# Mixture of experts on one core: Gelus kept in PSUM, a list made from fewer sequences, no GpSimd drain, stores between loads

## The chip, the cores and the metric

The kernel runs on one core of a Trainium2 chip. The metric is the device time of one execution in microseconds. All times below are of one core.

## The reference

32 sequences of 128 tokens, each token a row of 128 numbers, pass through two layers, and x is added at the end.

```python
# layer 1, conditioned on the sequence
h = gelu(x @ fc1_w.T + fc1_b)                    # 128 -> 512
shared = h @ fc2_w.T + fc2_b                     # 512 -> 96
expert_x = h @ experts_w[indices].T + experts_b  # 512 -> 32, one of 16 experts per sequence
y = concatenate([shared, expert_x])
# layer 2, conditioned on the token
scores = y @ router_w.T                          # 8 experts
top_v, top_i = top_k(scores, 2); routing_w = softmax(top_v)
for e in range(8):
    w_e = sum(where(top_i == e, routing_w, 0))
    out = out + (gelu(y @ expert_w1[e].T) @ expert_w2[e].T) * w_e
return x + out
```

All is float32; the Gelus are exact ones.

## The kernel before

**Pieces.** Layer 1 and the routing run over 16 pieces of two sequences. Per piece TensorE multiplies up (`up`), ScalarE makes the Gelu, TensorE multiplies down, DVE adds the biases (`y_first`), TensorE turns and scores, DVE finds the two best experts (`choose`, `mark`), and `place_pairs` gives each of the two copies of a row its slot in the DRAM tensor `slots`, where every expert has a room of its own. GpSimd writes the rows to their slots, four indirect transfers (scatters) a piece, 64 in all (L519).

**Tiles.** Layer 2 runs over 23 tiles of rows that all belong to one expert: 16 wide ones of 512 rows and 7 narrow ones of 256, in the order wide 0 to 11, narrow 12 and 13, wide 14 to 17, narrow 18 to 22. Which expert and which slots a tile has is found at run time by DVE, in lists: the first three tiles come from the first list, made when 10 pieces are placed, the next four from the second, made on 14 pieces (28 sequences), the rest from the third, made on all. `LIST_PIECE` and `LIST_WIDE` hold these numbers. `early_counts` and `early_list` make the first two lists, `last_counts`, `last_list`, `narrow_list`, `own_tiles`, `needed_tiles` and `counted_signals` the later ones, as chains of small DVE operations placed between the tiles' work (tiles 2, 3, 4, 5, 6 to 9 and 10).

**SP's queue** fetches: for each tile the rows (`pick`, from `slots`) and the expert's weights (`load_weights`, SBUF to SBUF, four buffers), in order. Before the first pick of a list it waits until the scatters of that list's pieces have landed. It writes the eight fillers (rows behind each expert's last one) in threes behind tiles 4, 5 and 6, and the first pick of the third list waits for all of them.

**One tile.** float32 products are made of three passes of float32r: each operand is split into a high and a low part, on both sides. `turn_in` transposes the picked rows into PSUM; ScalarE casts the high part (`picked_high`), DVE subtracts it for the low one (`picked_low`). `tile_up(t, g)` fills half g of `hp` (PSUM, two halves of 1024 columns), six matmuls of 512 columns. ScalarE makes the Gelu from hp into `hs_raw` in SBUF (`tile_gelu`), casts its high part into `hs` (`tile_high`), DVE subtracts it from hs_raw for the low part (`tile_low`, L854). `tile_down` multiplies down, again in halves. DVE copies the result (`flat`), TensorE turns it (`turn_out`), DVE scales the rows by the routing weight (`rows_of`), and GpSimd scatters them into the DRAM tensor `results` (L527), four scatters for a wide tile and two for a narrow one. The last three tiles take one pass and ScalarE does flat and rows_of.

TensorE's order in tile t: up(t, 0), turn_in(t + 1), down(t - 1, 0), up(t, 1), turn_out(t - 2), down(t - 1, 1). DVE's: flat(t - 2), low(t - 1, 1), picked_low(t + 1), low(t, 0), rows_of(t - 2), then a piece of list work. All engines run in written order.

**The end.** In eight chunks SP loads the two results of each token into z when the scatters that this chunk needs have landed (counted at run time, `load_chunk`), DVE adds both and x, SP stores (`store_chunk`). Seven loads come first, then four stores, the eighth load, and the other stores. Then SP waits for all stores and scatters, and all engines meet at a barrier, ahead of which each one drains.

## Time and profile before

| | us |
|---|---|
| median of 3 runs | 238.14 (237.66 to 239.77) |
| the profiled execution | 237.69, its span 235.7 |
| TensorE busy | 203.8 (86%) |
| weight loads of TensorE | 175.3 (74%) |
| DVE busy | 166.6 (71%) |
| ScalarE busy | 143.4 (61%) |
| GpSimd busy | 166.9 (71%) |
| chain that ended last | GpSimd 35%, DVE 20%, issue 19%, TensorE 15%, DMA 6% |

The span is what the profiler sees from the first to the last instruction; the time of the execution is 2.0 us longer. Busy shares leave out the issue of DMAs, and GpSimd's work here is mostly the issue of scatters: between two of them stand some 0.3 us in which the profile names nothing ("issue"). A line of the timeline gives start and length, the engine, the line of the kernel, what is written and read, and in brackets how long the engine stood idle before it and what ended that. PE is TensorE, ACT is ScalarE, POOL is GpSimd, SPq is SP's queue. Matmuls overlap: the start of the next one tells more than a length.

### The profile page before, as it was taken

To read this page: it belongs to the slowest core of one execution; us is meant where nothing else is said; L and a number is where in the kernel's file an instruction comes from. 1 tells how busy PE (TensorE), PEld (TensorE's weight loads), DVE (VectorE), ACT (ScalarE), POOL (GpSimd) and SP (SyncE) were. 2 spreads that over 40 slices of the span, in tenths; PEclk is the share of its full clock that TensorE was granted. 3 is DMA by queue.
4 is the path that set the end of the run, shared out by engine and by line. 5 is a ranking of instruction groups with operands and counts; after the bars stand their busy time and mean duration, and the time that the engine had idled before them with its cause. 6 is when DMAs were issued, how large, how long until landed. Compare 5 with 4: busy or idle time off the path is not lost.

```text
span 235.7 us, 4056 instructions
## 1 busy us (share of the span) xinstructions
PE 203.8 (86%) x1259; PEld 175.3 (74%) x1259; DVE 166.6 (71%) x558; ACT 143.4 (61%) x259; POOL 166.9 (71%) x180
## 2 busy tenths in 40 slices
PE   7999999998898684699999999999999999798200
PEld 3899999997797463588878888888978889686100
DVE  1269999998766883359999999997587666455520
ACT  3768978875556745246776666776569764554200
POOL 5437777877777777745766877787777778777730
PEclk9999999999999999599999999999999999999955
DMA  5899793532278811997849777657897589978970
GB/s 172 248 319 285 233 286 95 136 118 85 87 272 278 318 60 34 332 343 271 330 161 356 268 271 254 255 185 250 298 375 266 217 279 332 394 236 253 313 255 0
DMA packets 25799, 56.11 MB, mean 238 GB/s; under 512 B 4872, under 2 KB 11280, under 8 KB 23218
## 3 DMA queue, kind: packets, MB, share of 16 engines
q1 hardware_dynamic: 20800, 47.27, 58.6%
q0 software_dynamic: 4544, 8.54, 10.4%
q8 instruction: 10, 0.16, 0.3%
q10 hardware_dynamic: 434, 0.06, 0.2%
q14 instruction: 11, 0.09, 0.1%
HBM read 22.76 MB, written 13.02 MB: 152 GB/s over the span
## 4 chain that ended last, share of the span: by engine, by line
POOL 35%; DVE 20%; issue 19%; PE 15%; DMA 6%; SPq 1%; POOLq 0%; DVEq 0%
POOL results L527 25%; POOL slots L519 10%; PE dd L983 5%; PE hp L966 3%; DVE hs L854 2%; DVE ffn L841 2%; DMA results<-rows,back_row 2%; DMA z<-results 2%; PE hp L969 2%; PE hp L1010 1%; DVE top_exp L692 1%; DMA picked<-slots 1%; PE misc L1043 1%; DVE rows L867 1%; DMA slots<-y_rows,slot 1%
## 5 line engine op out<-in xcount | busy, mean ns | idle before, releaser
L527 POOL DMA_INDIRECT results<-rows,back_row x78 | 94.1, 1206 | 31.1 <-issue 23.7
L519 POOL DMA_INDIRECT slots<-y_rows,slot x64 | 66.9, 1045 | 25.7 <-issue 18.9
L1033 PE MATMUL hp<-xs,w 128*128 128x512 f32 x192 | 50.5, 398 | 1.6 <-DVE xs L848 1.6
L854 DVE TENSOR_TENSOR hs<-hs_raw,hs 128x1024 fp32r<-128x1024 f32 x36 | 43.9, 1221 | 10.0 <-ACT hs L596 9.8
L588 ACT ACTIVATE hs_raw<-hp 128x1024 f32<-128x1024 f32 x32 | 32.8, 1025 | 29.3 <-PE hp L1033 29.3
L1033 PEld LDWEIGHTS hp<-xs,w 128*128 128x128 f32 x192 | 36.2, 191 | 9.9 <-issue 2.0
L596 ACT ACTIVATE hs<-hs_raw 128x1024 fp32r<-128x1024 f32 x36 | 38.2, 1061 | 0.6
L983 PE MATMUL dd<-cond,hs_raw 128*128 128x128 f32 x256 | 35.5, 282 | 0.0
L983 PEld LDWEIGHTS dd<-cond,hs_raw 128*128 128x128 f32 x256 | 31.6, 192 | 0.3 <-issue 0.2
L545 ACT ACTIVATE hs_raw<-hp,fc_bias 128x256 f32<-128x256 f32 x64 | 26.0, 468 | 4.1 <-PE hp L969 2.2
L1043 PE MATMUL misc<-hs,w 128*128 128x512 f32 x96 | 27.4, 423 | 0.0
L1043 PE MATMUL dd<-hs,w 128*128 128x512 f32 x96 | 26.1, 407 | 1.0 <-DVE hs L854 1.0
L966 PE MATMUL hp<-xs,w 128*128 128x256 f32 x168 | 25.8, 295 | 0.0
L966 PEld LDWEIGHTS hp<-xs,w 128*128 128x128 f32 x168 | 21.7, 189 | 0.0
L1043 PEld LDWEIGHTS dd<-hs,w 128*128 128x128 f32 x96 | 16.9, 189 | 4.4 <-DVE hs L854 1.4
L1043 PEld LDWEIGHTS misc<-hs,w 128*128 128x128 f32 x96 | 17.7, 198 | 3.1
L584 ACT ACTIVATE xs<-dd 128x512 fp32r<-128x512 f32 (+1 forms) x20 | 11.0, 551 | 11.6 <-PE dd L1018 11.5
L1018 PE MATMUL dd<-ident,picked 128*128 128x128 f32 x64 | 10.2, 284 | 5.5 <-DMA picked<-slots 5.4
L1089 PE MATMUL tr<-ident,yT 128*128 128x128 f32 x78 | 12.4, 274 | 2.3 <-ACT yT L603 2.3
L572 ACT ACTIVATE y_rows<-gap 128x2 f32<-128x2 f32 x32 | 4.8, 197 | 15.3 <-DVE gap L697 15.3
L1089 PEld LDWEIGHTS tr<-ident,yT 128*128 128x128 f32 x78 | 9.6, 140 | 5.9 <-ACT yT L603 3.5
L1018 PEld LDWEIGHTS dd<-ident,picked 128*128 128x128 f32 x64 | 8.0, 145 | 7.7 <-DMA picked<-slots 6.1
(154 smaller groups left out, 294.2 us busy)
## 6 DMA issues: line engine op xcount, KB each, us to landing
w<-ffn SPq DMA_DIRECT2D x20, 1024.0 KB, 5.3
picked<-slots SPq DMA_DIRECT2D x16, 264.0 KB, 3.2
ffn_raw<-in_wT SPq DMA_DIRECT2D x8, 512.0 KB, 5.8
z<-results SPq DMA_DIRECT2D x8, 512.0 KB, 4.9
cond<-in_cexpT SPq DMA_DIRECT2D x32, 80.0 KB, 2.4
x_rows<-in_x SPq DMA_DIRECT2D x1, 2048.0 KB, 11.7
out<-z SPq DMA_DIRECT2D x8, 256.0 KB, 4.6
xs_raw<-in_xT SPq DMA_DIRECT2D x7, 256.0 KB, 5.1
```

The source lines that it names most:

```text
L519: pool.indirect_dma_start(out=slots, out_offset=bass.IndirectOffsetOnAxis(ap=slot[:, p, n:n + 1], axis=0), in_=y_rows[:, p % YB, k, r, :], ...
L527: pool.indirect_dma_start(out=results, out_offset=bass.IndirectOffsetOnAxis(ap=back_row[:, t, r:r + 1], axis=0), in_=rows[:, t % RB, r, :] ...
L545: act.activation(hs_raw[:, p % 2, 1, g, cols], hp[:, g, cols], ACT.Gelu, bias=fc1_bias[:, f:f + 1]).then_inc(a_gelu, 1)
L588: act.activation(hs_raw[:, (NP + t) % 2, 1, g, :], hp[:, g, :], ACT.Gelu).then_inc(c_gelu, 1)
L596: act.activation(hs[:, (NP + t) % 2, 0, g, :], hs_raw[:, (NP + t) % 2, 1, g, :], ACT.Copy)\
L854: dve.tensor_tensor(hs[:, u, 1, g, :], hs_raw[:, u, 1, g, :], hs[:, u, 0, g, :].bitcast(F32), ALU.subtract).then_inc(c_lo, 1)
L966: mm = pe.matmul(to, fc1_parts[:, part, f * P:(f + 1) * P], xs[:, c % XB, v, at:at + PER * P], start=m == 0, stop=m == 2)
L983: mm = pe.matmul(dd[:, p % 2, r, :], hs_raw[:, p % 2, 1, g, n * TILE + r * P:n * TILE + (r + 1) * P], weights_at(p, r)[:, :, f, :], start= ...
L1018: mm = pe.transpose(dx[:, r * P:(r + 1) * P], rows_in(t)[:, r, 0:P], ident[:, :])
L1033: mm = pe.matmul(hp[:, g, n * TILE:(n + 1) * TILE], w[:, t % WB, 0, part, f * P:(f + 1) * P], xs[:, (NP + t) % XB, v, :], start=m == 0, st ...
L1043: mm = pe.matmul(results_of[t % 2], w[:, t % WB, 1, part, f * P:(f + 1) * P], hs[:, (NP + t) % 2, v, g, n * TILE:(n + 1) * TILE], start=f ...
L1089: mm = pe.transpose(tr[:, r, :], yT[:, r * P:(r + 1) * P], ident[:, :])
```

## The change

1. The Gelus of tiles 1 to 19 are written back into `hp` instead of into `hs_raw`; `tile_high` and `tile_low` read them there. Tile 0 and the last three still go to SBUF. TensorE may overwrite a half of hp when the low part of the tile before is made (`c_lo`), not when its Gelu is (`c_gelu`).
2. The three passes of a product are taken with the high parts of both sides first; a group starts on the high part of its input and waits for the low part ahead of its third matmul.
3. The block is left without a drain of GpSimd.
4. The second list is made from 13 pieces (26 sequences) in place of 14, and has 3 tiles in place of 4; the third has one more. The first two lists are made ahead of `choose` within a piece, the second one in pieces 14 and 15 in place of after the last. The fillers move one tile earlier.
5. Stores 0 to 3 are issued each after loads 4 to 7.
6. Smaller moves: DVE makes low(t, 0) of a wide tile ahead of picked_low, and of a narrow tile behind rows_of; ScalarE makes high(t, 0) ahead of picked_high.

```diff
-LIST_PIECE = (LAST - 6, LAST - 2, LAST)
-LIST_WIDE = (3, 4, 9)
+LIST_PIECE = (LAST - 6, LAST - 3, LAST)
+LIST_WIDE = (3, 3, 10)
...
+        def up_of(t, g):
+
+            return hp[:, g if wide(t) else t % 2, :]
+
+
+        def gelu_of(t, g):
+            return hs_raw[:, (NP + t) % 2, 1, g, :] if t == 0 or t >= BY_ACT else up_of(t, g)
...
-        block_ctx = ctx.enter_context(nc.Block())
+        block_ctx = ctx.enter_context(nc.Block(no_gpsimd_drain=True))
...
-                    if t == 4:
+                    if t == LIST_START[1]:
                         sp.wait_ge(s_end, 1)
                         sp.sem_inc(s_go, 1)
                         ends_at = registers(end_i[0:1, :], 0, (EXP - 1) * ROOM * UNIT + TOKENS)
-                    if 4 <= t <= 6:
-                        for e in range((t - 4) * 3, min((t - 3) * 3, EXP)):
+                    if n == 1:
+                        for e in range((t - LIST_START[1]) * 3, min((t - LIST_START[1] + 1) * 3, EXP)):
                             write_filler(ends_at[e], e)
...
-            for c in range(CHUNKS - 1):
+
+            for c in range(CHUNKS):
                 load_chunk(c)
-            for c in range(CHUNKS // 2):
-                store_chunk(c)
-            load_chunk(CHUNKS - 1)
+                if c >= CHUNKS // 2:
+                    store_chunk(c - CHUNKS // 2)
             for c in range(CHUNKS // 2, CHUNKS):
                 store_chunk(c)
...
             def tile_gelu(t, g):
                 act.wait_ge(c_up, gelus(t, g))
-                act.activation(hs_raw[:, (NP + t) % 2, 1, g, :], hp[:, g, :], ACT.Gelu).then_inc(c_gelu, 1)
...
+                act.activation(gelu_of(t, g), up_of(t, g), ACT.Gelu).then_inc(c_gelu, 1)
 
             def tile_high(t, g):
                 act.wait_ge(c_gelu, gelus(t, g))
-                act.activation(hs[:, (NP + t) % 2, 0, g, :], hs_raw[:, (NP + t) % 2, 1, g, :], ACT.Copy)\
-                   .then_inc(c_hi, 1)
+                act.activation(hs[:, (NP + t) % 2, 0, g, :], gelu_of(t, g), ACT.Copy).then_inc(c_hi, 1)
...
                 if wide(t):
                     tile_gelu(t, 0)
+                    tile_high(t, 0)
                     picked_high(t + 1)
-                    tile_high(t, 0)
                     tile_gelu(t, 1)
                     tile_high(t, 1)
...
-                dve.tensor_tensor(hs[:, u, 1, g, :], hs_raw[:, u, 1, g, :], hs[:, u, 0, g, :].bitcast(F32),
+                dve.tensor_tensor(hs[:, u, 1, g, :], gelu_of(t, g), hs[:, u, 0, g, :].bitcast(F32),
                                   ALU.subtract).then_inc(c_lo, 1)
...
+                for i in (0, 1):
+                    if p == LIST_PIECE[i] + 2:
+                        early_counts(i)
+                    if p == LIST_PIECE[i] + 3:
+                        early_list(i)
                 if p:
                     choose(p - 1)
                     mark(p - 1)
-                if p == LIST_PIECE[0] + 2:
-                    early_counts(0)
-                if p == LIST_PIECE[0] + 3:
-                    early_list(0)
 
             y_first(LAST)
             picked_low(0)
             place_pairs(LAST - 1)
             choose(LAST)
             mark(LAST)
-            early_counts(1)
+            picked_low(1)
+            tile_low(0, 0)
             place_pairs(LAST)
             dve.tensor_copy(end_i[:, :], run[:, NP, :]).then_inc(s_end, 1)
-            picked_low(1)
-            early_list(1)
-            tile_low(0, 0)
             tile_low(0, 1)
...
                 if wide(t - 1):
                     tile_low(t - 1, 1)
+                if wide(t):
+                    tile_low(t, 0)
                 if t + 1 < BY_ACT:
                     picked_low(t + 1)
-                tile_low(t, 0)
                 if t - 2 < FREE:
                     rows_of(t - 2)
+                if not wide(t):
+                    tile_low(t, 0)
...
-            PASSES = ((0, 1), (1, 0), (0, 0))
+
+            PASSES = ((0, 0), (1, 0), (0, 1))
...
             def tile_up(t, g):
                 if g == 0:
-                    pe.wait_ge(c_xlo, t + 1)
-                    if t - 1 == LATE_WIDE:
-                        pe.wait_ge(c_gelu, gelus(t - 1, 0))
-                elif t:
-                    pe.wait_ge(c_gelu, last_gelu(t - 1))
+                    pe.wait_ge(c_xhi, t + 1)
+                if t == 1:
+                    pe.wait_ge(c_gelu, gelus(0, g))
+                elif t and wide(t - 1):
+                    pe.wait_ge(c_lo, gelus(t - 1, g))
...
                     for m, (part, v) in enumerate(PASSES):
+                        if f == 0 and m == 2:
+                            pe.wait_ge(c_xlo, t + 1)
...
             def tile_down(t, g):
-                pe.wait_ge(c_lo, gelus(t, g))
+                pe.wait_ge(c_hi, gelus(t, g))
                 for n in range(GB):
                     f = g * GB + n
                     for m, (part, v) in enumerate(PASSES):
+                        if n == 0 and m == 2:
+                            pe.wait_ge(c_lo, gelus(t, g))
...
                             weights_of(t + 2)
-                        if g == 1 and n == 0 and m == 1:
-                            pe.wait_ge(c_gelu, gelus(t + 1, 0))
...
             def narrow_up(t):
-                pe.wait_ge(c_xlo if t < BY_ACT else c_xhi, t + 1)
+                pe.wait_ge(c_xhi, t + 1)
+                if wide(t - 1):
+                    pe.wait_ge(c_lo, gelus(t - 1, 0))
...
             tile_up(0, 0)
-            rank(LAST)
             turn_in(1)
             tile_up(0, 1)
+            rank(LAST)
             weights_of(1)
-            pe.wait_ge(c_gelu, 1)
             tile_up(1, 0)
```

SP's queue at the second list, from its wait for the scatters (s_spread) on. Before:

```order
L301 TENSOR_LOAD list_i [waits s_spread12,s_spread13,s_spread11,s_list,s_spread10]
L339 ISA
L339 DMA picked<-slots 128x528
L352 ISA [waits a_up]
L352 DMA w<-ffn 128x2048
L339 ISA
L339 DMA picked<-slots 128x528
L352 ISA [waits c_down]
L352 DMA w<-ffn 128x2048
L301 TENSOR_LOAD end_i [waits s_end]
```

And now:

```order
L305 TENSOR_LOAD list_i [waits s_spread12,s_spread11,s_list,s_spread10]
L343 ISA
L343 DMA picked<-slots 128x528
L356 ISA [waits a_up]
L356 DMA w<-ffn 128x2048
L305 TENSOR_LOAD end_i [waits s_end]
L325 ISA
L325 DMA slots<-filler 128x264
L325 ISA
L325 DMA slots<-filler 128x264
L325 ISA
L325 DMA slots<-filler 128x264
```

The wait for piece 13 is gone from the second list, and the first three fillers stand between the fetches of tile 3 and those of tile 4.

DVE in wide tile 2, up to its scaling of tile 0's rows. Before:

```order
L860 COPY yT<-dd 128x512 [waits c_down]
L854 TENSOR_TENSOR hs<-hs_raw,hs 128x1024 [waits c_hi]
L846 COPY back_row<-picked 128x4 [waits c_xhi]
L848 TENSOR_TENSOR xs<-dd,xs 128x512
L854 TENSOR_TENSOR hs<-hs_raw,hs 128x1024 [waits c_hi]
L867 TENSOR_TENSOR rows<-tr,picked 128x512 [waits c_turn]
```

And now:

```order
L859 COPY yT<-dd 128x512 [waits c_down]
L853 TENSOR_TENSOR hs<-hp,hs 128x1024 [waits c_hi] x2
L845 COPY back_row<-picked 128x4 [waits c_xhi]
L847 TENSOR_TENSOR xs<-dd,xs 128x512
L866 TENSOR_TENSOR rows<-tr,picked 128x512 [waits c_turn]
```

The two low parts (hs) now follow each other, read hp in PSUM and no longer hs_raw in SBUF, and the next tile's rows (xs) come behind them.

TensorE in a wide tile: the second half-up, the turn-out and the second half-down. Before:

```order
L1033 MATMUL hp<-xs,w 128x512 [waits c_gelu]
L1033 MATMUL hp<-xs,w 128x512 x5
L1089 MATMUL tr<-ident,yT 128x128 [waits c_flat]
L1089 MATMUL tr<-ident,yT 128x128 x3
L1043 MATMUL misc<-hs,w 128x512 [waits c_lo]
L1043 MATMUL misc<-hs,w 128x512 [waits s_w3]
L1043 MATMUL misc<-hs,w 128x512 [waits c_gelu]
L1043 MATMUL misc<-hs,w 128x512 x3
```

And now:

```order
L1037 MATMUL hp<-xs,w 128x512 [waits c_lo]
L1037 MATMUL hp<-xs,w 128x512 x5
L1099 MATMUL tr<-ident,yT 128x128 [waits c_flat]
L1099 MATMUL tr<-ident,yT 128x128 x3
L1049 MATMUL misc<-hs,w 128x512 [waits c_hi]
L1049 MATMUL misc<-hs,w 128x512 [waits s_w3]
L1049 MATMUL misc<-hs,w 128x512 [waits c_lo]
L1049 MATMUL misc<-hs,w 128x512 x3
```

The half-up waits for the low part of the tile before instead of its Gelu; the half-down starts on the high part.

## Rows read from the trace of the kernel before

**Rows 1.** The chain of waits from 83 to 96.5: start, length (us), what held it.

```profile
83.70 0.96 POOL slots L519
...
89.25 2.28 DMA slots<-y_rows,slot
...
93.70 2.66 DMA picked<-slots
```

**Rows 2.** The timeline, TensorE: start, length, engine, line, operation, count, idle before.

```profile
89.45 1.52 PE L1033 MATMUL hp<-xs,w 128*128 128x512 f32 x6
...
96.41 1.11 PE L1018 MATMUL dd<-ident,picked 128*128 128x128 f32 x4 [5.44 <-DMA picked<-slots]
...
103.72 0.62 PE L1033 MATMUL hp<-xs,w 128*128 128x512 f32 x2
```

**Rows 3.** Stretches: length, busy time of each engine, TensorE's granted clock, DMA share, GB/s.

```profile
90.00:100.00 10.00, 4.56 (x16) 3.48 (x15) 3.19 (x5) 2.98 (x4) 7.87 (x8) 0.72 0.59 203
```

**Rows 4.** The timeline in a steady tile: DVE, ScalarE and TensorE.

```profile
129.71 1.55 PE L1033 MATMUL hp<-xs,w 128*128 128x512 f32 x6
...
131.47 1.22 DVE L854 TENSOR_TENSOR hs<-hs_raw,hs 128x1024 fp32r<-128x1024 f32 x1
...
132.70 1.06 ACT L596 ACTIVATE hs<-hs_raw 128x1024 fp32r<-128x1024 f32 x1
...
132.93 1.55 PE L1033 MATMUL hp<-xs,w 128*128 128x512 f32 x6
...
134.32 0.60 PE L1089 MATMUL tr<-ident,yT 128*128 128x128 f32 x4
...
136.14 0.62 PE L1033 MATMUL hp<-xs,w 128*128 128x512 f32 x2
```

**Rows 5.** The timeline: subtractions on DVE, and scatters of GpSimd that start inside them.

```profile
86.31 0.68 DVE L848 TENSOR_TENSOR xs<-dd,xs 128x512 fp32r<-128x512 f32 x1
86.32 0.96 POOL L519 DMA_INDIRECT slots<-y_rows,slot  x1 [0.31 <-issue]
...
133.79 1.23 DVE L854 TENSOR_TENSOR hs<-hs_raw,hs 128x1024 fp32r<-128x1024 f32 x1 [0.18 <-ACT hs L596]
133.99 1.89 POOL L527 DMA_INDIRECT results<-rows,back_row  x1 [0.30 <-issue]
```

**Rows 6.** The timeline and then the chain of waits, near the end.

```profile
198.74 1.22 DVE L854 TENSOR_TENSOR hs<-hs_raw,hs 128x1024 fp32r<-128x1024 f32 x1 [1.51 <-ACT hs L596]
...
201.34 0.98 POOL L527 DMA_INDIRECT results<-rows,back_row  x1 [0.52 <-issue]
...
217.12 5.32 DMA results<-rows,back_row
```

**Rows 7.** The last barrier's line: durations in ns, then the start in us.

```profile
L112 POOLq DRAIN  x1: 11092/11092/11092, 224.4 to 224.4; - x1
...
L112 SPq DRAIN  x1: 7/7/7, 230.4 to 230.4; - x1
```

**Rows 8.** The timeline of SP's queue around the fillers.

```profile
95.46 0.81 SPq L352 DMA_DIRECT2D w<-ffn  x1
98.86 3.06 SPq L321 DMA_DIRECT2D slots<-filler  x3
...
111.76 1.39 SPq L321 DMA_DIRECT2D slots<-filler  x2
120.34 0.35 SPq L339 DMA_DIRECT2D picked<-slots  x1
```

**Rows 9.** The timeline: low parts on DVE beside second halves on TensorE.

```profile
106.76 1.22 DVE L854 TENSOR_TENSOR hs<-hs_raw,hs 128x1024 fp32r<-128x1024 f32 x1
106.93 1.55 PE L1033 MATMUL hp<-xs,w 128*128 128x512 f32 x6
...
119.81 1.55 PE L1033 MATMUL hp<-xs,w 128*128 128x512 f32 x6
...
120.49 1.22 DVE L854 TENSOR_TENSOR hs<-hs_raw,hs 128x1024 fp32r<-128x1024 f32 x1
```

More of the change, by code:

```diff
@@ L96, in gelus @@
     return sum(2 if wide(i) else 1 for i in range(t)) + g + 1
-def last_gelu(t):
-    return gelus(t, 1 if wide(t) else 0)
 def wait(eng, sem, value):
@@ L587, in tile_gelu @@
                 act.wait_ge(c_up, gelus(t, g))
-                act.activation(hs_raw[:, (NP + t) % 2, 1, g, :], hp[:, g, :], ACT.Gelu).then_inc(c_gelu, 1)
-            def narrow_gelu(t):
-                act.wait_ge(c_up, gelus(t, 0))
-                act.activation(hs_raw[:, (NP + t) % 2, 1, 0, :], hp[:, t % 2, :], ACT.Gelu).then_inc(c_gelu, 1)
+                act.activation(gelu_of(t, g), up_of(t, g), ACT.Gelu).then_inc(c_gelu, 1)
             def tile_high(t, g):
                 act.wait_ge(c_gelu, gelus(t, g))
-                act.activation(hs[:, (NP + t) % 2, 0, g, :], hs_raw[:, (NP + t) % 2, 1, g, :], ACT.Copy)\
-                   .then_inc(c_hi, 1)
+                act.activation(hs[:, (NP + t) % 2, 0, g, :], gelu_of(t, g), ACT.Copy).then_inc(c_hi, 1)
             def flat(t):
@@ L645, in _ @@
                     picked_high(t + 1)
-                    narrow_gelu(t)
+                    tile_gelu(t, 0)
                     tile_high(t, 0)
@@ L649, in _ @@
                     flat(t - 2)
-                    narrow_gelu(t)
+                    tile_gelu(t, 0)
                     rows_of(t - 2)
@@ L1063, in narrow_up @@
                         for m, (part, v) in enumerate(PASSES):
+                            if f == 0 and m == 2:
+                                pe.wait_ge(c_xlo, t + 1)
                             mm = pe.matmul(narrow_block(hp[:, t % 2, :], f), w[:, t % WB, 0, part, f * P:(f + 1) * P],
@@ L1071, in narrow_down @@
             def narrow_down(t):
-                pe.wait_ge(c_lo if t < BY_ACT else c_gelu, gelus(t, 0))
+                pe.wait_ge(c_hi if t < BY_ACT else c_gelu, gelus(t, 0))
                 for f in range(FB):
@@ L1075, in narrow_down @@
                         for m, (part, v) in enumerate(PASSES):
+                            if f == 0 and m == 2:
+                                pe.wait_ge(c_lo, gelus(t, 0))
                             mm = pe.matmul(results_of[t % 2][:, 0:UNIT], w[:, t % WB, 1, part, f * P:(f + 1) * P],
```

## The prediction, made before the changed kernel was run

> **What bounds the kernel now.** I read the chain of waits first. It is mostly GpSimd: back to back scatters of pieces, then a hop over SP and a pick, then tiles, then back to back scatters of results. Three places decide, and I opened the timeline at each.
>
> First, the middle. The 56th of the 64 slot scatters begins at 89.25, lands 2.28 us later, and SP issues the pick of tile 3 at 93.70, 4.45 us after that scatter began [rows 1]. TensorE has finished the first half of tile 2 at 91.0 and sits idle until 96.41, when tile 3 is there [rows 2]. In the stretch from 90 to 100 its granted clock averages 0.72 [rows 3]; so in part of it the clock stood at the lower of its two levels (1.2 of 2.4 GHz), after a pause of 5.4 us.
>
> Second, the steady tiles. TensorE starts one tile at 129.71, its second half at 132.93 and the next tile at 136.14: 3.22 and 3.21 us, 6.43 a tile, with no pause named between [rows 4]. That is TensorE's own work, so DVE and ScalarE are free there until they are late. GpSimd also takes 6.4 a tile, but not by its own work: a scatter costs 0.98 plus 0.30 of issue [rows 5, 6], and 4 x 1.28 = 5.1. The scatter that starts at 133.99, inside the DVE subtraction of 133.79 to 135.02, takes 1.89 [rows 5]: it ends 0.86 after the subtraction does. The scatter at 86.32 starts inside a subtraction too, but one that reads PSUM (xs from dd), and takes 0.96 [rows 5]. So a DVE operation whose two inputs lie in SBUF holds a scatter up, one with an input in PSUM does not. The Trainium skill (SBUF — State Buffer, SBUF: two separate sides) says the same: VectorE with two SBUF inputs and GpSimd exclude each other on a shared port pair. By that rule, the trace agrees.
>
> Third, the end. The last scatter that a load of z waits for starts at 217.12 and needs 5.32 us to land while stores run; then come a load of z, two additions and one store [rows 6]. SP is through with everything at 230.4, but the span ends at 235.7: GpSimd's DRAIN, 11.09 us long, began at 224.4 and holds the last barrier until 235.5 [rows 7].
>
> **The change, part by part.** The sum is made against the profiled execution, 237.69 us (span 235.7 and 2.0 around it); the median of the runs is 0.45 higher.
>
> *No drain of GpSimd.* SP's own end becomes the end: 235.7 to about 230.5, so 5.2 us. All results have landed by then, since SP waits for them. Bounds: 0, if whatever GpSimd does in those 11 us is waited for elsewhere, and 5.2.
>
> *Second list on 26 sequences.* SP waits for the 52nd scatter in place of the 56th: 83.70 against 89.25 [rows 1], 5.55 us. That scatter is not earlier through anything else, as GpSimd runs back to back before it. It may be later: tile 0 keeps its Gelu in SBUF, and its two all-SBUF subtractions now lie before the 52nd scatter. A start that falls into one waits for up to 1.0, on average half. I take 0.95 for both together (0 to 1.9). Tile 3 then arrives 4.6 us earlier, at 91.8. Will TensorE be there? It is at 91.0 now [rows 2], which is already soon enough. It should be there 1 to 2 us sooner (an estimate), since DVE no longer makes the 19 list operations between the pieces and tile 0's low parts; they go into the last two pieces, partly into waits that DVE has there. So it waits 1 to 3 us instead of 5.4.
>
> *The clock.* From 96.41 to 103.72 stand 7.31 us [rows 2] for a tile less its first half-up; at the full clock that work takes 6.43 - (134.32 - 132.93) = 5.04 [rows 4]. If the shorter pause leaves the clock up, 2.3 us are gained. I take the whole, as 1 to 3 us of idling are much less than the 5.4 before which it fell; the bound is 0.
>
> *The fillers one tile earlier.* They now sit between the pick of tile 3 and that of tile 4 in SP's queue. Three take 3.06 us [rows 8], with the register loads ahead of them 2.6. Pick 4 falls to 6.8 us behind pick 3, and lands about 0.4 after TensorE wants it. The first pick of the third list before came 8.6 us after the last fillers began (111.76 to 120.34) [rows 8]; by the same step it is now some 0.4 late as well. Both lie in front of a larger stall of the same tile (next part), so 0, with up to 1 on the path if transfers are slow.
>
> *Gelus stay in PSUM.* The half of hp is free only when its low part is done: gelu, high, low instead of gelu alone. For g = 0: high runs from 132.70 to 133.76 and low takes 1.22, so the half would be free at 135.0 and is wanted at 136.14 [rows 4]; high also moves ahead of the cast of the next tile's rows. Slack 1.2 or more. For g = 1 DVE's place in line decides. In a steady tile its low ended at 131.47 + 1.22 = 132.69, and the half is wanted at 132.93 [rows 4]: slack 0.24, so about 0.1 in each of four such tiles. Where DVE makes lists in between there is none. Counting for the last list pushed the low of tile 2 to 107.98, and tile 3's second half started at 106.93: 1.05 us of stall now [rows 9]. The narrow list pushed it to 121.71 against 119.81: 1.9 [rows 9], of which some 0.25 were paid before, when the half-down behind it waited for the same low part, so 1.65. The signal counts of tile 10 are like a shorter list, 0.5; the first late wide tile has the same race, 0.2. Sum of losses 3.8, bounds 2 and 6. How long gelu and high take on PSUM is in no row of these; the nearest is high from SBUF to SBUF, 1.06 [rows 4], and I keep that. The 512 wide subtraction from PSUM takes 0.68 [rows 5]; twice that, 1.36, counts its fixed part twice and is the upper bound for the low part, the present 1.22 is the lower, and I take 1.22. The Trainium skill (VectorE: DVE Perf Modes, the TRN2 errata) puts a PSUM source 62 cycles above an SBUF source, 0.065 us; by it the three list tiles would lose some 0.3 us more.
>
> *High parts first* lets a group start two matmuls before the low part is there. A busy TensorE gains nothing from it. The added waits in mid-group cost nothing when they are met: the half whose down has three waits takes 3.21, the half whose down has one 3.22 [rows 4].
>
> *GpSimd set free.* Until tile 15 its scatters only keep pace with TensorE. At the end they decide. Eleven steps lie between the scatters at 201.34 and 217.12 [rows 6]; at 1.28 each they are 14.1, not 15.8. The first starts about 1.5 earlier, since in narrow tiles rows_of now stands ahead of the low part (198.74, 1.22 long, with DVE idle for 1.51 ahead of it) [rows 6]. Less 0.6 for the z additions, which are still all in SBUF: 2.6 us, bounds 1 and 3.5.
>
> *Stores between loads.* Four stores stand in SP's queue between the seventh load and the eighth, beside the scatter whose landing takes 5.32 where one of a slot took 2.28 [rows 1, 6]. Three of them now go earlier, between loads. I take 0.8 (0 to 2.5). Each store waits for an addition three loads back, which was done before; nothing is held.
>
> Sum: 5.2 + 4.6 + 2.3 - 3.8 + 2.6 + 0.8 = 11.7; 237.69 - 11.7 = 226.0, and 226.4 on the scale of the median.
>
> **Rivals.**
> (a) *The clock falls again* in the remaining pause, or scatters collide with tile 0's subtractions in full: 2.3 or a little more is missing, 228.7. For it speaks that a pause of 1 to 3 us is left, with shorter ones just ahead of it; against it, that this is little more than half of the 5.4 at most.
> (b) *The drain is only moved.* GpSimd has work for 9 us after its last scatter, and the program's end may wait for that outside the span: 5.2 missing, 231.6. Nothing in the trace tells.
> (c) *The loop over PSUM becomes the bound*, and the kernel ends slower. For g = 0 the slack is 1.2. To eat the 11.7 over 14 wide tiles, each must lose 0.85, so gelu, high and low together must be 2.05 us longer, 0.7 each on 1.0 to 1.2. The row of a PSUM read (0.68 for 512) speaks against it. At 0.5 each it is 0.3 a tile, 230.5; at 0.8 each it is 1.2 a tile, 243 and slower than before.
> (d) *TensorE gains more than I give*: no list stalls as DVE's idle moments absorb them, and stores help fully: 222.5.
>
> **How the numbers follow.** Forecast 0.55, (a) 0.18, (b) 0.12, (c) 0.06, of which half above 237, (d) 0.09. Its own bounds make the forecast 223.5 to 229. The range takes in (a), (b) and the edge of (d): 222.5 to 231.5. A measurement of this kernel can tell about 1% from no change. Within 1% needs (b) with most of (c): 0.03. Slower 0.03. Faster 0.94.
>
> **What would show each step.** Page: no DRAIN row on GpSimd at the end, and SP's end at the span's end. Timeline: pick of tile 3 near 89, TensorE's transposes of it near 91.8, and a granted clock near 1.00 from 90 to 100. Low parts read hp; scatters from tile 1 on take 0.98 except beside all-SBUF operations, and GpSimd shows idle time waiting for rows. TensorE's waits name DVE's low part before an up: twice over 1 us, at tiles 3 and 5. I am wrong if TensorE's tile takes clearly more than 6.43, if the time around the span grows past 2.0, or if the pause before tile 3 is over 4 us.

## The result and the profile after

The changed kernel takes 228.09 us, the median of four executions (226.1 to 228.23); the kernel before, run beside it, 238.83. The ratio is 0.953, 95% interval 0.947 to 0.958. The profiled execution took 226.10 us against 237.69 before, its span 224.2 against 235.7. The forecast was 226.4, with a range of 222.5 to 231.5 and 0.94 for faster; made against the profiled execution it was 226.0, and that execution took 226.1. Executions of a kernel fall into a fast and a slow state: the ratios, and the medians of the experiments below, are of fast ones, and a ratio is not the plain quotient of two medians.

The head of the page and its chain, of the kernel after:

```profile
span 224.2 us, 4074 instructions
PE 204.3 (91%) x1259; PEld 174.4 (78%) x1259; DVE 166.0 (74%) x558; ACT 143.1 (64%) x259; POOL 150.0 (67%) x180
...
PE 43%; POOL 26%; issue 10%; DVE 10%; DMA 7%; ACT 2%; SPq 1%; POOLq 0%; DVEq 0%
```

TensorE has as much work as before (204.3 us) in a shorter span. GpSimd lost 17 us of busy time (150.0 from 166.9), and TensorE now leads the chain with 43% where it had 15%.

The chain of waits of the kernel after, from the 52nd scatter to tile 3; it answers to [rows 1]:

```profile
83.68 2.27 DMA slots<-y_rows,slot
...
86.11 1.36 SPq L305
...
87.65 2.82 DMA picked<-slots
```

The scatter that SP waits for starts at 83.68, where that scatter already was in the kernel before (83.70), and tile 3 is on TensorE at 90.51 where it was at 96.41. TensorE's timeline there, for [rows 2]:

```profile
88.52 1.62 PE L1037 MATMUL hp<-xs,w 128*128 128x512 f32 x6 [0.60 <-DVE hs L853]
90.51 0.66 PE L1020 MATMUL dd<-ident,picked 128*128 128x128 f32 x4 [0.37 <-DMA picked<-slots]
...
95.57 1.54 PE L1037 MATMUL hp<-xs,w 128*128 128x512 f32 x6
...
99.89 1.65 PE L1037 MATMUL hp<-xs,w 128*128 128x512 f32 x6 [0.94 <-DVE hs L853]
...
114.40 1.66 PE L1037 MATMUL hp<-xs,w 128*128 128x512 f32 x6 [1.06 <-DVE hs L853]
...
153.91 1.65 PE L1037 MATMUL hp<-xs,w 128*128 128x512 f32 x6 [0.56 <-DVE hs L853]
```

The pause is 0.37 us long in place of 5.44, and from 90.51 to 95.57 stand 5.06 us in place of 7.31. The stretch that answers to [rows 3] has the whole clock:

```profile
90.00:100.00 10.00, 8.69 (x44) 6.83 (x44) 7.17 (x23) 7.08 (x8) 7.68 (x8) 1.00 1.02 367
```

The row at 99.89 is the other side. What held it shows on DVE, in the timeline:

```profile
94.99 0.16 DVE L766 TENSOR_TENSOR count<-run,room 128x8 f32<-128x8 f32 x1
...
98.02 0.69 DVE L859 COPY yT<-misc 128x512 f32<-128x512 f32 x1
98.62 2.35 DVE L853 TENSOR_TENSOR hs<-hp,hs 128x1024 fp32r<-128x1024 f32 x2
```

From 94.99 to 98.0 DVE counts for the last list, then comes a copy, and only then the low part that frees half of hp. It ends at about 99.8 and TensorE goes on at 99.89. Over the whole kernel the waits of TensorE read:

```profile
PE hp L1037 <- DVE hs L853: 3.2, 4, 1.1
```

These are the four rows above. The first, 0.60 in tile 2, costs nothing, since TensorE then waits for tile 3's rows anyway. The other three, in tiles 3, 5 and 11, make 2.6 us. The weight loads ahead of them wait too, so the tiles lose more: tile 3 takes 1.2 us more than in the kernel before, tile 4 0.3, tile 5 1.1, tiles 6 to 10 together 0.3 and tile 11 0.8. The steps of tiles 6 to 10 are 6.43 to 6.58 us.

The end, in the chain of waits and in SP's timeline, for [rows 6]:

```profile
210.43 5.73 DMA results<-rows,back_row
...
216.21 4.05 DMA z<-results
```

```profile
209.80 0.36 SPq L448 DMA_DIRECT2D z<-results  x1
210.21 0.46 SPq L452 DMA_DIRECT2D out<-z  x1
210.77 0.37 SPq L448 DMA_DIRECT2D z<-results  x1
211.20 0.54 SPq L452 DMA_DIRECT2D out<-z  x1
216.21 0.36 SPq L448 DMA_DIRECT2D z<-results  x1
```

The last barrier, for [rows 7]; there is no row of GpSimd any more, and SP's stands at the end of the span:

```profile
L108 SPq DRAIN  x1: 7/7/7, 223.9 to 223.9; - x1
```

From the two profiles the 11.5 us of span divide like this:

| place | rows of before, after | gain, us | forecast |
|---|---|---|---|
| tile 3 is turned in | 96.41, 90.51 | 5.9 | 4.6 |
| tile 3 to the next tile's start (clock) | 7.31, 5.06 | 2.25 | 2.3 |
| that start to the first narrow tile | 57.89, 61.65 | -3.8 | -3.8 |
| from there to the last scatter that a load waits for | 55.51, 53.21 | 2.3 | 2.6 |
| its landing | 5.32, 5.73 | -0.4 | +0.8 |
| load, additions, last store | 7.96, 7.74 | 0.2 | 0 |
| SP's end to the end of the span | 5.3, 0.3 | 5.0 | 5.2 |

The third line runs from 103.72 to 161.61 before and from 95.57 to 157.22 after. Each line is a difference of two starts in two executions; another execution of the same kernel moves a line by some tenths, the landing by more.

### The profile page after: what moved, and what is told of

It reads as the page before. It is cut to its first block, busy times and chain, and to the rows that moved or that the text cites. A ratio compares the mean times of both kernels' runs of the same rounds, so it can differ in the third digit from the quotient of the medians.

```text
span 224.2 us, 4074 instructions
## 1 busy us (share of the span) xinstructions
PE 204.3 (91%) x1259; PEld 174.4 (78%) x1259; DVE 166.0 (74%) x558; ACT 143.1 (64%) x259; POOL 150.0 (67%) x180
## 4 chain that ended last, share of the span: by engine, by line
PE 43%; POOL 26%; issue 10%; DVE 10%; DMA 7%; ACT 2%; SPq 1%; POOLq 0%; DVEq 0%
POOL slots L523 24%; PE hp L1037 14%; PE dd L1049 7%; PE misc L1049 7%; PE tr L1099 3%; PE hp L1072 3%; DMA results<-rows,back_row 3%; DVE hs L853 2%; PE dd L1020 2%; POOL results L531 2%; PE hp L971 2%; DMA z<-results 2%; PE hp L1012 1%; PE dd L1086 1%; PE dd L985 1%
## 5 line engine op out<-in xcount | busy, mean ns | idle before, releaser
L531 POOL DMA_INDIRECT results<-rows,back_row x78 | 78.5, 1007 | 41.4 <-DVE rows L866 20.8
L523 POOL DMA_INDIRECT slots<-y_rows,slot x64 | 65.5, 1023 | 25.8 <-issue 18.9
L1037 PE MATMUL hp<-xs,w 128*128 128x512 f32 x192 | 52.0, 407 | 3.2 <-DVE hs L853 3.2
L592 ACT ACTIVATE hp<-hp 128x1024 f32<-128x1024 f32 x34 | 34.3, 1010 | 28.7 <-PE hp L1037 28.7
L853 DVE TENSOR_TENSOR hs<-hp,hs 128x1024 fp32r<-128x1024 f32 x34 | 41.3, 1219 | 12.5 <-ACT hs L596 12.4
L596 ACT ACTIVATE hs<-hp 128x1024 fp32r<-128x1024 f32 x34 | 34.9, 1027 | 1.1
L1049 PE MATMUL misc<-hs,w 128*128 128x512 f32 x96 | 26.2, 408 | 0.0
L1049 PEld LDWEIGHTS misc<-hs,w 128*128 128x128 f32 x96 | 16.8, 189 | 2.9
L866 DVE TENSOR_TENSOR rows<-tr,picked 128x512 f32<-128x512 f32 x16 | 11.0, 686 | 6.3 <-PE tr L1099 6.3
L943 DVE TENSOR_TENSOR z<-z 128x512 f32<-128x512 f32 x8 | 5.5, 692 | 9.7 <-DMA z<-results 9.7
```

The costliest lines, as they stand in the source:

```text
L523: pool.indirect_dma_start(out=slots, out_offset=bass.IndirectOffsetOnAxis(ap=slot[:, p, n:n + 1], axis=0), in_=y_rows[:, p % YB, k, r, :], ...
L531: pool.indirect_dma_start(out=results, out_offset=bass.IndirectOffsetOnAxis(ap=back_row[:, t, r:r + 1], axis=0), in_=rows[:, t % RB, r, :] ...
L592: act.activation(gelu_of(t, g), up_of(t, g), ACT.Gelu).then_inc(c_gelu, 1)
L596: act.activation(hs[:, (NP + t) % 2, 0, g, :], gelu_of(t, g), ACT.Copy).then_inc(c_hi, 1)
L853: dve.tensor_tensor(hs[:, u, 1, g, :], gelu_of(t, g), hs[:, u, 0, g, :].bitcast(F32), ALU.subtract).then_inc(c_lo, 1)
L1037: mm = pe.matmul(hp[:, g, n * TILE:(n + 1) * TILE], w[:, t % WB, 0, part, f * P:(f + 1) * P], xs[:, (NP + t) % XB, v, :], start=m == 0, st ...
```

## The experiments

again, drain, sbuf_late and sbuf_early ran on one chip, where the kernel before took 238.61. The others ran in three groups on three other chips, where it took 261.8, 268.5 and 265.9. What was different there is told with nodrain. The changed kernel itself was run only where the kernel before takes 238 us.

**again: the changed kernel once more.**

> The changed kernel once more, beside which the others of this group are read. All theories: 226 to 228 us, 0.953 of the kernel before. If the 2 us between its fast and its slow executions have a place in the trace, a second profile may show it: the start of tile 3 (90.51 us in the first profile), or the landing of the last scatter (5.73 us).

227.55 us, ratio 0.952 (0.947 to 0.958): the same. It executed in 225.4 to 228.4, so a single execution says no more than some 1.5 us to either side. Its profiled execution (227.63) shows a wait that the first one had almost without:

```profile
PE dd L1020 <- DMA picked<-slots: 2.2, 2, 2.0
```

TensorE was ready for tile 3 2.0 us early and stood still for that long, yet tile 3 came at 90.67, and the granted clock from 90 to 100 was 1.00 again. In sbuf_early below the pause was 2.96 us, with the same 1.00. In the kernel before the clock fell inside the pause of 5.44 and was 0.50 from 95 to 101.

Why the pause was 0.37 in one profile and 2.03 in the other shows earlier, where TensorE makes the halves of tile 0. The stretch from 78 to 81, the first profile and then again:

```profile
78.00:81.00 3.00, 3.00 (x10) 2.42 (x10) 0.97 (x4) 2.33 (x5) 2.09 (x3) 0.50 1.01 416
```

```profile
78.00:81.00 3.00, 3.00 (x17) 2.08 (x16) 1.25 (x3) 2.98 (x4) 2.39 (x3) 1.00 0.89 361
```

In the first profile the clock fell here, though from 66 on TensorE had stood still for no more than 0.58 us at a time. Tile 2 was turned in 1.8 us later than in again (83.21, 81.42), of which 0.4 were there before the fall. The pause ahead of tile 3 took that up, so tile 3 came no later for it. sbuf_late has the same fall, from about 77 to 80; drain and sbuf_early have not. So a short pause ahead of tile 3 doesn't by itself promise the whole clock: what made it fall at 78 stays open.

**drain: the changed kernel with GpSimd's drain.**

```diff
-        block_ctx = ctx.enter_context(nc.Block(no_gpsimd_drain=True))
+        block_ctx = ctx.enter_context(nc.Block())
```

> The changed kernel with the drain of GpSimd put back. Theory (the drain only held the last barrier): the span is 5.0 us longer than that of the changed kernel, since SP was done at 230.4 of 235.7 before and is done at 223.9 of 224.2 now. Rival (GpSimd's work after its last scatter is waited for anyway, outside the span): the time is the same and only the part outside the span, 1.9 us, shrinks.

232.86 us, ratio 0.976 (0.971 to 0.981), 5.3 above again. Its last barrier:

```profile
L108 POOLq DRAIN  x1: 10837/10837/10837, 218.9 to 218.9; - x1
...
L108 SPq DRAIN  x1: 7/7/7, 224.6 to 224.6; - x1
```

SP is through at 224.6 and GpSimd's row lasts until 229.7, with the span's end at 230.0. The drain is wholly at the end and does nothing that anyone waits for: shown.

**sbuf_late: Gelus in SBUF, TensorE's waits as in the changed kernel.** It undoes the place alone.

```diff
-            return hs_raw[:, (NP + t) % 2, 1, g, :] if t == 0 or t >= BY_ACT else up_of(t, g)
+            return hs_raw[:, (NP + t) % 2, 1, g, :]
```

> The changed kernel with all Gelus in SBUF again, and every wait as in the changed kernel (TensorE still waits for the low part). So only the place of the Gelu differs. Theory (two SBUF inputs on DVE hold a scatter up): the 78 scatters of results take 94 us in sum, not 78.5, GpSimd no longer waits for rows (20.8 us now), and the end is 1 to 2 us later, as the lag of GpSimd counts only at the end. Rival 1 (scatters are slowed by the transfers they compete with, not by DVE): 78 to 80 us in sum as now. Rival 2 (GpSimd's pace bounds the whole stretch): 6 us or more later.

228.25 us, ratio 0.956 (0.951 to 0.961): 0.7 above again, with intervals that overlap. The scatters of results, on the page of sbuf_late and then of the changed kernel:

```profile
L531 POOL DMA_INDIRECT results<-rows,back_row x78 | 91.3, 1171 | 28.0 <-issue 21.3
```

```profile
L531 POOL DMA_INDIRECT results<-rows,back_row x78 | 78.5, 1007 | 41.4 <-DVE rows L866 20.8
```

A scatter is issued in 1.17 us on average instead of 1.01, 13 us in all. The timelines show it one by one, sbuf_late first:

```profile
132.54 1.22 DVE L853 TENSOR_TENSOR hs<-hs_raw,hs 128x1024 fp32r<-128x1024 f32 x1
132.75 1.86 POOL L531 DMA_INDIRECT results<-rows,back_row  x1 [0.30 <-issue]
```

```profile
127.83 1.22 DVE L853 TENSOR_TENSOR hs<-hp,hs 128x1024 fp32r<-128x1024 f32 x1 [0.47 <-ACT hs L596]
128.67 0.98 POOL L531 DMA_INDIRECT results<-rows,back_row  x1 [0.30 <-issue]
```

Inside a subtraction of two SBUF inputs the scatter lasts until 134.61, 0.85 after the subtraction; inside one that reads hp it takes its 0.98. The one edit between the two kernels is where the Gelu lies, so the stretching is shown to come from it. In time the two kernels differ by less than their executions spread: the intervals leave room for some 2 us, and exclude the 6 of the second rival. Most of the 13 us turns into idle time: GpSimd waits 20.8 us for DVE's rows in the changed kernel and 4.9 in sbuf_late.

**sbuf_early: Gelus in SBUF, and TensorE waits for the Gelu only.** The edit of sbuf_late, and with it

```diff
-                if t == 1:
-                    pe.wait_ge(c_gelu, gelus(0, g))
-                elif t and wide(t - 1):
-                    pe.wait_ge(c_lo, gelus(t - 1, g))
+                if t:
+                    pe.wait_ge(c_gelu, gelus(t - 1, g if wide(t - 1) else 0))
...
                 if wide(t - 1):
-                    pe.wait_ge(c_lo, gelus(t - 1, 0))
+                    pe.wait_ge(c_gelu, gelus(t - 1, 0))
```

> As the run before, and TensorE may overwrite a half of hp once the Gelu is read from it (c_gelu), as in the kernel before. Theory: the waits of TensorE for DVE's low part ahead of an up (3.2 us named, 3.8 by the starts of tiles 3 and 12) go, so tile 12 starts some 3.5 us earlier relative to tile 3; GpSimd, slowed to 6.4 us a tile, lags more at the end, so the time is 0 to 3 us below that of the changed kernel with its Gelus in SBUF. Rival (the stalls at tiles 3, 5 and 11 come from the fetches of rows and weights): tile 12 starts no earlier.

226.69 us, ratio 0.949 (0.944 to 0.954): no slower than again, 0.9 faster if anything. Its timeline, where tiles 4 and 13 are turned in:

```profile
97.24 0.27 PE L1020 MATMUL dd<-ident,picked 128*128 128x128 f32 x1
...
155.84 0.27 PE L1020 MATMUL dd<-ident,narrow_picked 128*128 128x128 f32 x1
```

These nine tiles take 58.60 us; in the changed kernel (96.96 to 158.66) 61.70, in again 62.01, in sbuf_late 62.04, and in the kernel before, which also waited for the Gelu only, 57.95. So the waits for the low part cost TensorE 3.1 to 4.1 us: shown, by the one edit between sbuf_late and sbuf_early and by the kernel before. The 58.60 even hold something else. TensorE waits 0.81 us for the rows of tile 6, turned in at 111.06, where the stalls of the other kernels hide that these rows are late.

The first narrow tile comes 2.8 us earlier than in the changed kernel (154.41, 157.22). GpSimd, with stretched scatters, gives 2.1 of that back until the scatter that the last load of z waits for (209.72, 210.43), and that scatter then takes 7.4 us to release the load, not 5.8. The last load goes out at 217.15, in the changed kernel at 216.21. Gelus in PSUM and Gelus in SBUF are thus two ways to the same end: the first costs TensorE, the second GpSimd. The changed kernel with its Gelus back in SBUF and TensorE's waits of before is as fast as it was, so the first item of the change earned no time that shows here.

**nodrain: the kernel before without the drain.**

```diff
-        block_ctx = ctx.enter_context(nc.Block())
+        block_ctx = ctx.enter_context(nc.Block(no_gpsimd_drain=True))
```

> The kernel before with the drain left out and nothing else. Theory (the drain is a fixed cost at the end, whatever stands ahead of it): minus 5.0 to 5.3 us, to about 233.4, ratio 0.978; the span ends less than 1 us after the last store, and no DRAIN row stands on GpSimd's queue. Rival (a part of the drain was only possible because something else of the change had already let GpSimd finish early): less than 4 us.

260.0 us against 261.8, ratio 0.989 (0.978 to 1.001): too uncertain to read as a size or to call a gain. Five us less would lie inside the interval, and so would no change. Its last barrier has no row of GpSimd and says

```profile
L112 SPq DRAIN  x1: 7/7/7, 259.1 to 259.1; - x1
```

in a span of 259.4. SP's end is the span's end once the drain is gone, as in the changed kernel; the size rests on drain alone.

On this chip and on the two of the later runs every kernel was slow, the kernel before too (23 to 30 us more than on the first chip). The trace shows how, but not why. Here ScalarE in stores:

```profile
194.28 1.03 ACT L597 ACTIVATE hs<-hp 128x1024 fp32r<-128x1024 f32 x1
203.17 0.60 ACT L589 ACTIVATE xs<-dd 128x512 fp32r<-128x512 f32 x1 [7.86 <-remote]
```

It stands for 7.86 us ahead of a cast whose input TensorE had made at 198.0 already. Such pauses of 1 to 8 us come on TensorE, ScalarE and DVE, most in the pieces, and the chain puts some 20% of the first 100 us down to "another core or an unknown queue", of which the profiles from the first chip have nothing. Their cause stays open. Medians of these runs compare programs that stand still in different places; steps between two rows of one stage without such a pause can still be read.

**stores: the changed kernel with the loads and stores in the order of before.**

```diff
-            for c in range(CHUNKS):
-                load_chunk(c)
-                if c >= CHUNKS // 2:
-                    store_chunk(c - CHUNKS // 2)
+            for c in range(CHUNKS - 1):
+                load_chunk(c)
+            for c in range(CHUNKS // 2):
+                store_chunk(c)
+            load_chunk(CHUNKS - 1)
```

> The changed kernel with the stores in the order of before: seven loads, four stores, the last load, four stores. Theory (the order at the end is worth little, since the last load waits for its scatter either way): the time stays within 0.8 us of the changed kernel's, above it if anything. Rival (stores between the loads take the memory from the last scatter, whose landing took 5.7 us in the changed kernel and 5.3 before): the time falls by 1 us or more, and the last load is released earlier behind its scatter.

269.2 us against 261.8, ratio 1.024 (1.011 to 1.038). The changed kernel wasn't run beside it, so that says nothing of the order of the stores; that question stays open. It says something of the rest: on this chip the change without its order of stores was slower than before. Its tiles 4 to 13 took 62.09 us, those of nodrain on the same chip 58.14, as the loss to the low parts would have it, and the earlier list had nothing to give back there, as list28 shows below.

**list28: the changed kernel with its second list put back on 28 sequences** (run three times, as list28, list28b and list28c).

```diff
-LIST_PIECE = (LAST - 6, LAST - 3, LAST)
-LIST_WIDE = (3, 3, 10)
+LIST_PIECE = (LAST - 6, LAST - 2, LAST)
+LIST_WIDE = (3, 4, 9)
...
-                for i in (0, 1):
+                for i in (0,):
...
             mark(LAST)
+            early_counts(1)
             picked_low(1)
...
             dve.tensor_copy(end_i[:, :], run[:, NP, :]).then_inc(s_end, 1)
+            early_list(1)
```

> The changed kernel with its second list put back: on the first 28 sequences, 4 tiles from it, made behind the last piece and the filler end as before; all else of the change stays. Theory (the forecast's first two terms are the list's): tile 3's turning in comes 5 to 6 us later (about 96), the low clock is seen again in the stretch between 90 and 100 us, and the time is 5 to 8 us above the changed kernel's 227.5. Rival (tile 3 came earlier because the multiplies no longer wait for the low parts, not because of the list): under 2 us.

> The kernel of list28, run again for the same reason. Theory (the forecast's first two terms, earlier rows and the clock, belong to the second list): tile 3's turning in comes 5 to 6 us later than in the changed kernel, the clock between 90 and 100 us is again below 0.8, and the time is 5 to 8 us above the changed kernel's 227.5. Rival (the new order of the products let tile 3 come early, not the list): under 2 us.

> The kernel of list28 a third time, for the case that the engines run without the pauses that the calls of list28 and list28b had in the pieces. Theory (the first two terms of the forecast belong to the second list): tile 3's turning in at 95 to 97 instead of 90.6, a granted clock below 0.8 between 90 and 100 us, and 5 to 8 us more than the changed kernel's 227.5: 233 to 235. Rival (the new order of the products let tile 3 come early): under 230. If the pauses are there again, before takes over 260 us, GpSimd has idle time before its 56th scatter, and the list costs nothing.

270.8 us beside 261.8 for before (ratio 1.036, 1.028 to 1.044); 268.5 beside 268.5; 266.8 beside 265.9 (1.017, 1.009 to 1.024). All three groups had the pauses, and the changed kernel did not run beside them, so neither the size of the list's term nor that of the clock's is tested. They do show on what the list's term hangs. GpSimd in list28c:

```profile
98.00 0.96 POOL L523 DMA_INDIRECT slots<-y_rows,slot  x1 [0.31 <-issue]
102.00 0.96 POOL L523 DMA_INDIRECT slots<-y_rows,slot  x1 [3.04 <-DVE slot L721]
...
105.78 0.96 POOL L523 DMA_INDIRECT slots<-y_rows,slot  x1 [0.30 <-issue]
```

The 52nd scatter is at 98.00 and the 56th at 105.78, with GpSimd waiting for slots in between, and TensorE turns tile 3 in only at 123.27, 17.5 us after that. TensorE isn't waiting for a pick there, but for its own work behind the pieces. The pieces are late, not the scatters, and four scatters less buy nothing. In the profile of the changed kernel, from 50 us to the last slot scatter at 99, GpSimd waits for anything but issue only once, for 0.3 us, and there the four scatters count.

**spread: the list arithmetic in single operations** (run three times, as spread, spread2 and spread3). The helpers hand over after each dependent operation; the same operations in the same order.

```diff
+GAP = {2: 8, 3: 8, 4: 4, 5: 4, 6: 4, 7: 3, 8: 2, 9: 2, 10: 2, 11: 2, 12: 2, 13: 2, 14: 2, 15: 2, 16: 2, 17: 2}
+END = {2: 5}
...
                 if wide(t - 1):
                     tile_low(t - 1, 1)
+                steps(GAP.get(t, 0))
                 if wide(t):
                     tile_low(t, 0)
...
-                if t == 2:
-                    last_counts()
-                if t == 3:
-                    last_list()
-                if t == 4:
-                    narrow_list()
...
+                steps(END.get(t, 0))
```

> The changed kernel with the list arithmetic of tiles 6 and later (last counts, last list, narrow list, needed tiles, counted signals) cut into single operations: eight of them ahead of the low parts of a tile's first half in tiles 2 and 3, two to four in tiles 4 to 17, in place of one block each behind tiles 2 to 10. Same operations, same order. Theory (3.8 us are lost because a block of 2 to 3 us stands between TensorE and the low parts that it needs): the waits of TensorE's first multiplies for the low parts shrink from 8 us over four waits to under 3, TensorE's stretch from tile 3 to the first narrow tile shortens by 3 to 4 us, and the time falls by 2.5 to 3.5 us, to about 224.5. Rival (GpSimd's scatters set the end of the middle tiles as well, so what TensorE gains waits there): TensorE's waits go but the last scatter comes less than 1 us earlier, and the time falls by under 1 us.

> The kernel of spread, run again, since in the call of nodrain, list28, spread and stores the engines stood still for 1 to 5 us at a time with no releaser in the trace while the pieces ran (before took 265 us there). Theory (3.8 us are lost to the list's blocks on VectorE): TensorE's tiles follow each other every 6.4 to 6.5 us from tile 3 to the first narrow tile, where the changed kernel had two steps of 7.6 and 7.8; its waits for the low parts are under 3 us in all; the time falls by 2.5 to 3.5 us against the changed kernel, to 224 to 225. Rival (GpSimd's scatters and their landings set the end, as in sbuf_early, where TensorE's 2.8 us bought nothing): TensorE's steps are regular and the last scatter comes less than 1 us earlier; the time falls by under 1 us.

> The kernel of spread a third time, for the same case. Theory (the list's blocks cost 3.8 us of TensorE and these come back): TensorE's steps from tile 3 to the first narrow tile are 6.4 to 6.5 us each, 58 to 59 us in all where the changed kernel had 61.1; the time is 224 to 225.5. Rival (GpSimd and the landings of its last scatters set the end): the same steps, but 227 or more.

262.6 us beside 261.8 for before (ratio 1.000, 0.994 to 1.006); 264.7 beside 268.5, from two executions each; 261.8 beside 265.9 (0.989, 0.982 to 0.996). In each group it was the fastest kernel with Gelus in PSUM: by 6.6 us against stores and 8.2 against list28, by 3.7 against list28b, by 5.0 against list28c. How much of that is pauses isn't known. The stage in question can be read, in the timeline of spread3:

```profile
128.73 0.27 PE L1070 MATMUL dd<-ident,picked 128*128 128x128 f32 x1
...
187.39 0.27 PE L1070 MATMUL dd<-ident,narrow_picked 128*128 128x128 f32 x1
```

Tiles 4 to 13 take 58.66 us, and in spread and spread2, with pauses among them, 59.95 and 59.86; in stores 62.09, in list28c 62.07, in list28 and list28b, with pauses, 64.05 and 64.36; in nodrain 58.14. TensorE's waits for low parts before an up were 2.4 us in spread, and in spread3

```profile
PE hp L1087 <- DVE hs L897: 1.4, 2, 0.8
```

So the stalls come from the blocks of list work and not from Gelus in PSUM as such: shown for TensorE's steps, 3.0 to 3.4 us of them. That the time falls by as much where the engines don't pause was not shown. GpSimd might let it, since in the changed kernel it waits 20.8 us for rows; but in sbuf_early 2.8 us of TensorE did not reach the end.

## Why the prediction came out right

**No drain, forecast 5.2.** Measured 5.0 in the profiles and 5.3 with drain. Rival (b), that the wait would only move, was wrong: outside the span stand 1.9 us, as before 2.0.

**Second list, forecast 4.6, measured 5.9.** The term was 5.55 less 0.95 for scatters that fall into tile 0's subtractions. Nothing of the 0.95 was left in the end: the 52nd scatter starts at 83.68 against 83.70 [rows 1]. One scatter ahead of it did start inside a subtraction of tile 0 (82.10, 1.28 long), but the scatters had come 0.34 earlier up to there. On top, the pick followed its scatter by 3.97, not 4.45 [rows 1], since SP read the list in 1.36 us and not in 1.81. The mechanism was right, the deduction too large. It also holds only where GpSimd runs back to back, as list28c shows. The prediction took that from the chain, as the state of the kernel, and didn't say that it is a condition.

**The clock, forecast 2.3, measured 2.25.** The clock was 1.00 from 90 to 100. The pause had been put at 1 to 3 us; it was 0.4 and, in again, 2.0, both without a fall. What the prediction didn't see is the fall at 78, with no pause over 0.58 ahead of it. It was harmless only because TensorE was early for tile 3.

**Fillers one tile earlier, forecast 0.** The pick of tile 4 came 4.5 us behind that of tile 3, not 6.8 as worked out, and TensorE didn't wait for it. The rows of tile 6 are the late ones, as forecast: hidden behind a stall in the changed kernel, 0.81 us of waiting in sbuf_early.

**Gelus in PSUM, forecast -3.8, measured -3.8.** The stalls stand where the lists are, as forecast, but the equal sum is partly luck. Tile 3 lost 1.2 where 1.05 was said, tile 5 1.1 where 1.65, tile 11 0.8 where 0.5, the steady tiles 0.3 where 0.4, and tile 4, behind the last list, 0.3 where nothing was said; the 0.2 for the first late wide tile lie outside this stretch. Comparing kernels gives 3.1 to 4.1. The fear that PSUM makes the three operations longer came to nothing: gelu takes 1.01 from hp to hp where it took 1.03 into SBUF, the high part 1.03 where it took 1.06, the low part 1.22 as before (means of the pages). By the table in the Trainium skill (VectorE: DVE Perf Modes, the TRN2 errata) the low part would be 0.065 us longer with a PSUM source, an estimate; this trace has 1219 ns against 1221 (means of 34 and 36), so no such surcharge shows on a 1024 wide subtraction. For ScalarE the same table of the Trainium skill has 52 cycles less with a PSUM source, by estimate 0.043 us; with that the trace agrees better, 1027 ns against 1061 for the high part.

**GpSimd set free, forecast 2.6, measured 2.3, but half of it for another reason.** The eleven steps up to the scatter that the last load waits for took 14.76 us, against 15.78 before and 14.1 + 0.6 in the forecast. The first of the twelve scatters starts 38.45 behind the first narrow tile instead of 39.73: 1.3, forecast 1.5. That 1.5 was put down to the new order in narrow tiles. sbuf_late and sbuf_early keep this order, with Gelus in SBUF, and there the distance is 39.5. So nearly all of it, too, came from the Gelus in PSUM. From the first narrow tile to the scatter in question stand 53.2 us in the changed kernel, 53.7 in again and 53.3 in drain, against 55.1 in sbuf_late, 55.3 in sbuf_early and 55.5 before. Little of it reaches the end, as the next point says.

**Stores between loads, forecast +0.8, measured -0.4: the mis-sized term.** The landing did not shorten. The rows say why the premise failed. In the kernel before, the scatter at 217.12 had these ahead of it and beside it in SP's timeline:

```profile
211.65 4.79 SPq L444 DMA_DIRECT2D z<-results  x4
216.49 3.59 SPq L448 DMA_DIRECT2D out<-z  x4
```

Now two loads and two stores go out between 209.80 and 211.20, around the scatter at 210.43. The four stores are gone from there, but loads that wait less have taken their place. In sbuf_late the same four go out late:

```profile
213.51 0.36 SPq L448 DMA_DIRECT2D z<-results  x1
213.92 0.46 SPq L452 DMA_DIRECT2D out<-z  x1
214.48 0.37 SPq L448 DMA_DIRECT2D z<-results  x1
214.91 0.57 SPq L452 DMA_DIRECT2D out<-z  x1
215.58 0.45 SPq L448 DMA_DIRECT2D z<-results  x1
```

The scatter at 212.41 has landed before 215.58, in 3.2 us at most. With the crowd beside it the time from the scatter's start to the load was 5.8 us in the changed kernel, 6.1 in again, 5.7 in drain and 7.4 in sbuf_early, though these four scatters start anywhere from 209.72 to 211.36. The last load goes out between 215.6 and 217.4 in all five kernels. This is read off several kernels, and no run changed the crowd alone where it could be timed; it fits, but isn't shown. It would explain why neither 13 us of GpSimd (sbuf_late) nor 2.8 us of TensorE (sbuf_early) moved the median by as much as 1 us.

**The whole.** 11.7 was summed and 11.6 measured, by errors that cancelled: 1.3 too little for the list, 1.2 too much for the landing. To meet it within 0.1 was luck, as the medians gain 10.7. The median lies 1.7 above the forecast because the profiled execution, against which the sum comes out, was the shortest of its four (the others 227.99 to 228.23), while the step from profile to median had been taken from before, where it was 0.45. Over all its runs the changed kernel's executions spread over 3 us.

## What to carry to other kernels

A buffer that comes free one engine later makes that engine's place in line part of the loop: look at what stands ahead of the freeing operation, above all at blocks of small dependent work, and cut those into pieces before or together with such a change. Count scatters on a list only where the chain shows that engine back to back up to that point. When two engines keep the same pace, relieving one at the other's cost brings nothing. And a last transfer that shares its way with loads and stores may land only when the crowd has passed, whenever it started; here that fits five profiles but isn't shown.

## What the runs showed of the chip

- GpSimd's drain at the end of a block took 10.8 to 11.1 us from GpSimd's last scatters on, and was worth 5.3 us here. Without it nothing else got longer.
- A scatter that starts inside a DVE operation with two SBUF inputs ended 0.85 us after that operation (1.86 for 0.98), as before; inside one that reads PSUM it lost nothing, even with its other input and its output in SBUF.
- ScalarE and DVE worked on PSUM at the pace of SBUF: 1.01 against 1.03 us for gelu on 1024 columns, 1.22 against 1.22 for the subtraction.
- TensorE kept its full clock over pauses of 0.4, 2.0 and 3.0 us ahead of tile 3. Within one of 5.4 it fell, to 0.50 from 95 to 101. It also fell to 0.50 from 78 to 81 in one of the two profiles of the changed kernel, where no pause ahead was over 0.58 us.
- On three other chips engines stood still for 1 to 8 us at a time with nothing in the trace to release them, and the kernel before took 10 to 13% longer. The gain of a change can vanish under that, since it moves what is waited for.
